# First layer of a graph network on one core: weights applied before the mixing over nodes, in another order of steps

## The reference, cut to what matters

```python
h = jnp.maximum(_layernorm(x, axis=-1), 0.0)
# first layer, W: (3, 128, 128)
adj_0 = jnp.diag(jnp.diagonal(adj))
adj_1 = jnp.triu(adj, k=1)
adj_2 = jnp.tril(adj, k=-1)
h = jnp.einsum('bjf,kfo->kbjo', x, W)
out = jnp.einsum('ij,bjo->bio', adj_0, h[0]) + jnp.einsum('ij,bjo->bio', adj_1, h[1]) \
    + jnp.einsum('ij,bjo->bio', adj_2, h[2])
return out + bias[None, None, :]
...
x = x + _L0_gnn_ref(h, L0_gnn_W, adj, L0_gnn_bias)
h = jnp.maximum(_layernorm(x, axis=-1), 0.0)
```

## Time and profile before

| | us |
|---|---|
| median of three runs | 1319.07 |
| the profiled execution | 1317.13 |
| its span, first to last instruction | 1315.4 |
| TensorE busy, whole span | 1214.1 |
| VectorE, ScalarE, GpSimd busy, whole span | 1018.3, 898.0, 325.0 |
| this stage: ScalarE's first instruction | at 30.82 |
| the next stage: ScalarE's first instruction | at 201.30 |

### The profile page before, as it was taken

How to read it: one execution, slowest core, us unless ns; L and a number is a source line. 1 busy time by engine, 2 the same in 40 slices (tenths; PEclk the granted TensorE clock), 3 DMA queues, 4 the chain that set the end, 5 groups by cost and what they waited for, 6 DMA issues and landing times. The chain is left out here.

```text
span 1315.4 us, 23598 instructions
## 1 busy us (share of the span) xinstructions
PE 1214.1 (92%) x6996; PEld 994.1 (76%) x6996; DVE 1018.3 (77%) x2037; ACT 898.0 (68%) x1681; POOL 325.0 (25%) x738
## 2 busy tenths in 40 slices
PE   2999988979979998899999999999998899978998
PEld 1989985643358886689879888987886677747998
DVE  4787766996768885988788879887775699976664
ACT  1766647857758886877687778777765799842332
POOL 3576750000057440000000000000000566633331
PEclk8999998998969999999999999999999799998999
DMA  7000000000031110000000000003000200000112
GB/s 298 1 0 0 0 0 0 0 0 0 0 137 64 64 57 1 0 1 1 1 0 1 0 1 1 1 1 128 1 1 33 97 0 1 1 0 33 73 73 81
DMA packets 14467, 37.90 MB, mean 29 GB/s; under 512 B 1856, under 2 KB 3904, under 8 KB 13120
## 3 DMA queue, kind: packets, MB, share of 16 engines
q1 hardware_dynamic: 13008, 36.31, 7.1%
q10 hardware_dynamic: 1392, 0.74, 0.2%
HBM read 20.27 MB, written 16.78 MB: 28 GB/s over the span
## 5 line engine op out<-in xcount | busy, mean ns | idle before, releaser
L955 ACT ACTIVATE gates<-bank,lstm_bias 128x512 f32<-128x512 f32 (+1 forms) x504 | 301.5, 636 | 101.5 <-PE bank L944 88.3
L139 ACT ACTIVATE l_h<-X,nmr,rstd 128x128 f32 (+1 forms) x512 | 210.1, 484 | 54.2 <-POOLq L133 32.8
L929 PE MATMUL bank<-lstm_node_hi,Wih_hi 128*128 128x512 f32 (+1 forms) x408 | 149.4, 366 | 0.0
L931 PE MATMUL bank<-lstm_node_lo,Wih_hi 128*128 128x512 f32 (+1 forms) x408 | 148.9, 365 | 0.0
L930 PE MATMUL bank<-lstm_node_hi,Wih_lo 128*128 128x512 f32 (+1 forms) x408 | 148.8, 365 | 0.0
L108 POOL TENSOR_TENSOR l2r_sum<-l2r_st 128x8 f32<-128x8 f32 x16 | 3.3, 208 | 532.2 <-DVE l2r_st L89 531.9
L940 PE MATMUL bank<-lstm_hid_hi,Whh_hi 128*128 128x512 f32 (+1 forms) x288 | 104.2, 362 | 4.5 <-DVE lstm_hid_hi L1011 4.3
L944 PE MATMUL bank<-lstm_hid_lo,Whh_hi 128*128 128x512 f32 (+1 forms) x288 | 106.8, 371 | 0.0
L941 PE MATMUL bank<-lstm_hid_hi,Whh_lo 128*128 128x512 f32 (+1 forms) x288 | 103.1, 358 | 0.0
L960 ACT ACTIVATE gates<-lstm_cell 128x512 f32<-128x512 f32 (+1 forms) x144 | 83.7, 581 | 21.6 <-DVE lstm_cell L998 21.3
L931 PEld LDWEIGHTS bank<-lstm_node_lo,Wih_hi 128*128 128x128 f32 x408 | 77.1, 189 | 11.7
(11 more groups left out here) (245 smaller groups left out, 3258.5 us busy)
## 6 DMA issues: line engine op xcount, KB each, us to landing
X<-in_x SPq DMA_DIRECT2D x8, 1024.0 KB, 14.1
x_spill<-X SPq DMA_DIRECT2D x32, 256.0 KB, 2.0
X<-x_spill SPq DMA_DIRECT2D x2, 4096.0 KB, 12.4
out<-X SPq DMA_DIRECT2D x32, 256.0 KB, 2.0
w_raw<-in_WihT SPq DMA_DIRECT2D x1, 1024.0 KB, 5.9
w_raw<-in_WhhT SPq DMA_DIRECT2D x1, 1024.0 KB, 8.1
W<-in_L_W ACTq DMA_DIRECT2D x1, 192.0 KB, 5.2
rows<-in_rows ACTq DMA_DIRECT2D x1, 128.0 KB, 4.4
```

The source lines that it names most:

```text
L139: last = act.activation(h[:, j, :], k.X[:, bass.ds(b0, TB), :][:, j, :], ACT.Relu, bias=k.nmr[:, bass.ds(b0, TB)][:, j:j + 1], scale=k.rst ...
L929: pe.matmul(out, hi, x_high, start=True, stop=False)
L931: last = pe.matmul(out, hi, x_low, start=False, stop=it.step == 0)
L955: act.activation(gate_of(it, g), k.bank[4 * s + g][:, 0:it.N], ACT.Tanh if g == GATE_G else ACT.Sigmoid, bias=k.lstm_bias[:, it.p - 1, g:g ...
```

## The change

The weights come first and the mixing over nodes second. TensorE transposes h; ScalarE takes the high part and VectorE the low part of the transposed h straight from PSUM (`hT_hi`, `hT_lo`). With the transposed h as the stationary operand, 12 float32r matmuls for each tile multiply it by all three weights side by side, 384 columns, into four PSUM banks (`psH`), of which there is one set. ScalarE copies them to SBUF (`H`) in two operations of 128x768 each. The mixing is then two float32 matmuls for a tile, 512 columns each, that is, over four batches at once. The diagonal's part is one `scalar_tensor_tensor` on VectorE with a scalar per node (`diag_col`), both of its large inputs in SBUF. `W` is split in high and low parts on VectorE ahead of the loop, in place of the adjacency. The work of each engine is written as one step for each tile t, with parts of neighbouring tiles in it; the loop covers a pair. GpSimd's list is unchanged.

```diff
@@ stage_setup
         def _(pe):
             pe.wait_ge(cst, 2)
-            pe.wait_ge(deg, 1)
-            pe.matmul(bank_dg[:, 0:P], onesPP[:, :], tmp[:, :], start=True, stop=True).then_inc(diag_ready, 1)
...
+            dve.wait_ge(deg, 4)
+            dve.tensor_copy(k.diag_col[:, :], rs[:, 2:3])
             dve.wait_ge(diag_ready, 1)
-            dve.tensor_copy(k.diag_bc[:, :], bank_dg[:, 0:P])
-            dve.wait_ge(diag_ready, 2)
@@ stage_layer0
+    psT, psO = k.bank[0:2], k.bank[6:8]
+    psH = k.psum[:, 2 * TW:6 * TW].rearrange("p (j c) -> p j c", j=TB)
...
+    FIRST = -2
+
+    def steps(eng, step):
+        for t in range(FIRST, 2 * S):
+            step(t // S, t % S, t)
+        with eng.Fori(2, n_it - 2) as i:
+            for s in range(S):
+                step(i, s, i * S + s)
+        for t in range(tiles - 2 * S, tiles + 2):
+            step(t // S, t % S, t)
...
         @block.scalar
         def _(act):
...
+            def step(i, s, t):
+                if there(t):
                     act.wait_ge(AB_ready[s], i + 1)
+                    if since(t, S):
+                        act.wait_ge(out_ready[s], i)
+                        act.wait_ge(H0_added[s], i)
+                    for j in range(0, TB, 2):
+                        last = act.activation(H[s][:, :, j:j + 2, :], psH[:, j:j + 2, 0:3 * P].rearrange("p j (k o) -> p k j o", k=3),
+                                              ACT.Copy)
+                    last.then_inc(H_ready[s], 1)
+                q, ahead = (s + 1) % S, i + (s + 1) // S
+                if there(t + 1):
+                    act.wait_ge(T_ready[q], ahead + 1)
+                    act.activation(hT_hi[q][:, :, :], as_tile(psT[q]), ACT.Copy).then_inc(hi_ready[q], 1)
+                if there(t + 2):
+                    x_ln.wait(act, s, i + 1)
+                    if since(t + 2, S):
+                        act.wait_ge(T_ready[s], i + 1)
+                    normalise_tile(act, k, h[s], (t + 2) * TB).then_inc(h_ready[s], 1)
...
         @block.tensor
         def _(pe):
...
+            def step(i, s, t):
+                q, ahead = (s + 1) % S, i + (s + 1) // S
+                if there(t + 1):
+                    pe.wait_ge(h_ready[q], ahead + 1)
+                    if since(t + 1, S):
+                        pe.wait_ge(lo_ready[q], ahead)
                     for j in range(TB):
+                        last = pe.transpose(psT[q][:, j * P:(j + 1) * P], h[q][:, j, :], k.ident[:, :])
+                    last.then_inc(T_ready[q], 1)
+                if there(t):
                     pe.wait_ge(lo_ready[s], i + 1)
+                    if since(t, 1):
+                        pe.wait_ge(H_ready[(s + 1) % S], i - (s + 1) % S + 1)
                     for j in range(TB):
+                        o = psH[:, j, 0:3 * P]
+                        pe.matmul(o, hT_hi[s][:, j, :], W_hi[:, :, :], start=True, stop=False)
+                        pe.matmul(o, hT_hi[s][:, j, :], W_lo[:, :, :], start=False, stop=False)
+                        last = pe.matmul(o, hT_lo[s][:, j, :], W_hi[:, :, :], start=False, stop=True)
                     last.then_inc(AB_ready[s], 1)
+                if there(t - 1):
+                    at = i - (s + 1) % S
+                    pe.wait_ge(H_ready[q], at + 1)
+                    if since(t - 1, S):
+                        pe.wait_ge(updated[q], at)
+                    pe.matmul(psO[q][:, :], k.A12T[:, 0, :], H[q][:, 0, :, :], start=True, stop=False)
+                    pe.matmul(psO[q][:, :], k.A12T[:, 1, :], H[q][:, 1, :, :], start=False, stop=True).then_inc(out_ready[q], 1)
...
         @block.vector
         def _(dve):
...
+            def step(i, s, t):
+                q, ahead = (s + 1) % S, i + (s + 1) // S
+                if there(t + 1):
+                    dve.wait_ge(hi_ready[q], ahead + 1)
+                    dve.tensor_tensor(hT_lo[q][:, :, :], as_tile(psT[q]), hT_hi[q][:, :, :].bitcast(F32),
+                                      ALU.subtract).then_inc(lo_ready[q], 1)
+                if there(t):
+                    dve.tensor_tensor(tile(t), tile(t), k.rows[:, R_L0:R_L0 + 1, :].broadcast_to([P, TB, P]),
                                       ALU.add).then_inc(biased[s], 1)
+                if there(t - 1):
+                    at = i - (s + 1) % S
+                    dve.wait_ge(out_ready[q], at + 1)
+                    dve.wait_ge(H0_added[q], at + 1)
+                    dve.tensor_tensor(tile(t - 1), as_tile(psO[q]), tile(t - 1), ALU.add).then_inc(updated[q], 1)
+                if there(t):
+                    dve.wait_ge(H_ready[s], i + 1)
                     dve.wait_ge(biased[s], i + 1)
+                    dve.scalar_tensor_tensor(tile(t), H[s][:, 2, :, :], k.diag_col[:, :], tile(t),
+                                             ALU.mult, ALU.add).then_inc(H0_added[s], 1)
+                if there(t - 1):
+                    dve.wait_ge(updated[q], at + 1)
+                    ln.stats(dve, tile(t - 1), q, at)
+                if there(t) and there(t + AHEAD * S):
+                    k.x_ln.stats(dve, tile(t + AHEAD * S), s, i + AHEAD)
...
```

More of the change, by code:

```diff
@@ L57, in each, with as_tile @@
     return [make(i) for i in range(n)]
+def as_tile(ps):
+    return ps[:, :].rearrange("p (b n) -> p b n", b=TB)
 class LayerNormTail:
@@ L180, in stage_setup @@
     dinv = sb("dinv", [P, 1])
-    bank_dg, bank_di = k.bank[0], k.bank[1]
+    bank_di = k.bank[1]
     with nc.Block() as block:
@@ L272, in stage_layer0 @@
     sem = lambda n: k.sem(n)
-    sb = lambda n, s: ctx.enter_context(nc.sbuf_tensor(n, s, F32))
+    sb = lambda n, s, t=F32: ctx.enter_context(nc.sbuf_tensor(n, s, t))
     h = each(S, lambda s: sb(f"l0_h{s}", [P, TB, P]))
[L275 to L286, removed]
@@ L287, in stage_layer0 @@
-    ln, x_ln, AHEAD = LayerNormTail(k, ctx, "l0", S), k.x_ln, k.X_AHEAD
-    n_it = k.B // TB // S
-    tile = lambda i, s: X[:, bass.ds((i * S + s) * TB, TB), :]
+    hT_hi, hT_lo = (each(S, lambda s: sb(f"l0_{n}{s}", [P, TB, P], F32R)) for n in ("hT_hi", "hT_lo"))
+    H = each(S, lambda s: sb(f"l0_H{s}", [P, 3, TB, P]))
+    W_hi, W_lo = (sb(f"l0_{n}", [P, 3, P], F32R) for n in ("W_hi", "W_lo"))
+    h_ready, T_ready, hi_ready, lo_ready, AB_ready, H_ready, H0_added, out_ready, biased, updated = (
+        each(S, lambda s: sem(f"l0_{n}{s}"))
+        for n in ("h", "T", "hi", "lo", "AB", "Hs", "H0", "out", "biased", "updated"))
@@ new lines, in stage_layer0 @@
+    W_ready = sem("l0_W")
+    psT, psO = k.bank[0:2], k.bank[6:8]
+    psH = k.psum[:, 2 * TW:6 * TW].rearrange("p (j c) -> p j c", j=TB)
+    ln, x_ln, AHEAD = LayerNormTail(k, ctx, "l0", S), k.x_ln, k.X_AHEAD
+    tiles = k.B // TB
+    n_it = tiles // S
+    there = lambda t: exists(t, tiles)
+    tile = lambda t: X[:, bass.ds(t * TB, TB), :]
+    FIRST = -2
[7 more added lines that the diff above has]
+            step(t // S, t % S, t)
@@ L306, in _ @@
         def _(act):
[L307 to L315, removed]
-                    act.wait_ge(AB_ready[s], i + 1)
[L317 to L320, removed]
@@ L322, in _ @@
-            normalise(0)
-            looped(act, n_it, turn)
+            def step(i, s, t):
+                if there(t):
+                    act.wait_ge(AB_ready[s], i + 1)
+                    if since(t, S):
[14 more added lines that the diff above has]
+                    normalise_tile(act, k, h[s], (t + 2) * TB).then_inc(h_ready[s], 1)
@@ L325, in _ @@
+            steps(act, step)
         @block.tensor
         def _(pe):
[L327 to L331, removed]
+            def step(i, s, t):
[4 more added lines that the diff above has]
+                        pe.wait_ge(lo_ready[q], ahead)
@@ L332, in _ @@
                     for j in range(TB):
-                        last = pe.transpose(psT[s][:, j * P:(j + 1) * P], h[s][:, j, :], k.ident[:, :])
-                    last.then_inc(T_ready[s], 1)
+                        last = pe.transpose(psT[q][:, j * P:(j + 1) * P], h[q][:, j, :], k.ident[:, :])
+                    last.then_inc(T_ready[q], 1)
+                if there(t):
                     pe.wait_ge(lo_ready[s], i + 1)
+                    if since(t, 1):
+                        pe.wait_ge(H_ready[(s + 1) % S], i - (s + 1) % S + 1)
@@ L353, in _ @@
+            pe.wait_ge(W_ready, 2)
+            steps(pe, step)
         @block.vector
         def _(dve):
[L355 to L366, removed]
-                                      ALU.add).then_inc(biased[s], 1)
[L368 to L372, removed]
-                    dve.wait_ge(biased[s], i + 1)
[L374 to L379, removed]
@@ L384, in _ @@
+            W = k.W0
+            for n, part in enumerate((1, 2, 0)):
+                last = dve.tensor_copy(W_hi[:, n, :], W[:, part, :])
+            last.then_inc(W_ready, 1)
+            dve.wait_ge(W_ready, 1)
+            for n, part in enumerate((1, 2, 0)):
```

(12 more changed lines are left out.)

3 lines of the change are left out of this document (removed).

## The result

The changed kernel takes 1429.19 us (median of four runs, 1427.18 to 1431.05) against 1317.87 for the kernel before beside it: a ratio of 1.084, with an interval of 1.082 to 1.087. It is slower by 111 us. The forecast was 1434, within 1396 to 1447.

A forecast was written before the change was run, and what follows sets the result against it. GpSimd's list was taken to bound the kernel at 10.14 us a pair; a closed loop at 17.6 us over thirteen pairs, plus prologue and tail, made the stage 115.3 us later: 1434 us, range 1396 to 1447.

The forecast's parts named there:

- What bounds the kernel before: In the stage before the change, GpSimd's list sets the turn of 10.14 us, though TensorE is busy 147.0 of 160.3 us.
- The closed loop: The coefficients' trip through GpSimd loses its turn of lead; a pair costs 15.3 to 15.8 us instead of 10.14.
- The loop at full clock: From the even tile's normalisation to the next even tile's, TensorE at 2.4 GHz: 15.3 to 15.8 us a pair.
- Which of 4.57 and 5.07: GpSimd's batch to ScalarE: 5.07 us if its last operation is held up beside VectorE's diagonal, else 4.57; pair 17.6 taken.
- The clock: TensorE idles 4.8 us a pair; T(4) and tile 3's matmuls then likeliest run at 1.2 GHz, adding 2.05 us.
- The sign for the clock: In the changed profile, PEclk drops to about 0.7 to 0.8 in slices 2 to 8.
- the second case: Clock holds or falls only now and then: 15.55 us a pair, 1406 us; sign PEclk at 9 or more; chance 0.27.
- The ends: Stage before N(4) and after N(30): N(4) at 60.2 us, the stage starting at 30.82; tail 22.9, then 4.7 us.
- The second rival: The batch comes in time and ScalarE's own chain binds: 6.41 us a tile, 12.8 a pair, 1365 us; chance 0.05.
- the third: Faster: both chains fit under GpSimd's list, its last operation not held up; 9.64 us a pair, 1311 us; chance 0.03.
- The other half: In the trace before, no TensorE idle shorter than 2.33 us lowered the clock, the longest of these being 1.67.

The follow-up runs named there:

- the shortened list: Kernel before with the power in GpSimd's coefficients behind the layer replaced by a multiplication, for the time alone: 1302.2 us, ratio 0.990.

## Why the prediction was right

- What bounds the kernel before: GpSimd's list, read from its 10.14 us turn without a foreign wait. Shown by the shortened list.
- The closed loop: shown both ways, by giving the lead back (54 us gained, 51 of them in the stage) and by taking it from the kernel before (120 us lost).
- The loop at full clock: 15.3 to 15.8 us for a pair. Keeping TensorE busy gave 15.8 in the pairs where the clock held and GpSimd's last operation was held up, and 15.37 in those where it was not and the low clock fell outside the trip. The settled terms in the trace after are 1.70 for 1.69 to the transposes, 1.40 for the copies, 0.64 for 0.66, 4.10 for 4.03, 0.18 for 0.16, and 4.99 for the batch.
- Which of 4.57 and 5.07: I took the middle. Beside the diagonal GpSimd's last operation took 0.65 us in place of 0.20, so the upper end was right, and so was the Trainium skill's rule (SBUF — State Buffer, Who interferes with whom). With TensorE kept busy it took 0.20 again in the pairs in which the diagonal came later.
- The clock: it fell in every pair, as forecast, but the step "It came back 4.2 us or more after work had resumed, in every one of them" was wrong, in the rows of before already. There the clock was 0.50 from 513.0 to 514.4 us and 1.00 from 514.5 to 516.0, so it came back 3.8 us after the matmul at 510.65; behind the idle stretch that ended at 1176.39 it came back after 3.7. In the kernel after, it came back some 5.3 us after the transposes of tile 4 and 4.4 us after those of tile 6, and these two pairs took 18.0 and 17.8 us where 17.6 was forecast. Later it came back sooner, some 2.8 us after the transposes at 165.90, so transposes to copies took 4.12 and not 4.83. The clock's share is 1.3 us in such a pair, not 2.05.
- The sign for the clock was badly chosen. PEclk stood at 0.88 over the stage where I had named 0.7 to 0.8, and its digit is 9 in four of the slices 2 to 8. By my words that would speak for the second case, in which the clock holds; the timelines show that it fell in every pair.
- The pair came out at 17.25 on average against 17.6: over the 13 pairs the clock's term was 0.6 too large, the batch's 0.2 too small. These two errors have opposite signs, so the total is closer than the terms are, and that much is luck.
- The ends: N(4) came 29.4 us into the stage (forecast 29.4), and 27.6 us lay between N(30) and the next stage (forecast 27.6). 13 x 0.35 = 4.6 us of the pairs is the difference between 1434 and 1429.
- The second rival, ScalarE's own chain of 6.41 a tile, was not what happened but was real: the lead alone ends on it at 6.38. So was the third: once the lead and ScalarE's order were both mended, the pair was 9.69 us for 9.64 and the kernel took 1310 us for 1311.

## What to carry to other kernels

When a loop is rewritten as steps of single tiles, follow each side chain (here statistics, coefficients, normalisation) from its producer's place in the step to its consumer's, and count how much of the lead is left; the same `AHEAD = 2` meant a turn of slack in one order and a closed loop in the other. Inside a step, put what other engines need for the next tile ahead of what waits for the current one. An engine with little busy time can set the pace when its list is a chain of short dependent operations: read its period, not its share.

## What the runs showed of the hardware that I had not expected

- How long TensorE idles does not alone decide whether the clock falls. In the kernel with the statistics first TensorE idled 2.65 and 1.89 us in turn and the clock stayed at 1.00 for 85 us. With three pairs of lead and no idle stretch above 1.9 us, it fell once in every two to four tiles, and with the added matmuls it fell too, in a pair in which the idle stretches are 0.96 and 1.89. So the forecast's reading that it falls behind every stretch above 2 us does not hold as a rule. The other half, that it falls behind none below 1.7, was not contradicted: with idle stretches of 1.41 us, in the kernel with the lead and the high part first, it stayed at 1.00 from 60 to 180 us.
- A pair of the kernel after settled at 17.04 to 17.15 us for the second half of the stage, and the one with ScalarE's order changed at 17.06 to 17.12, though their waits lie in different places. Whether that is more than chance is open; nothing here tried it.
